# Transposed-tile copies moved from ScalarE to VectorE in the attention stage, and two-bank PSUM tiles with paired GELUs in the first FFN stage

## The chip, the cores and the metric

The kernel runs on all 8 cores of one Trainium2 chip. The batch of 32 sequences is split into 4 per core, and the cores share nothing else than HBM. The metric is the device time in microseconds of the slowest core. A core has five engines that run side by side: TensorE (PE, with its weight loads shown as PEld), VectorE (DVE), ScalarE (ACT), GpSimd (POOL, here only a queue for DMAs) and SyncE (SP, also a queue for DMAs). They order each other by semaphores.

## The reference

For x of shape (32, 2048, 1024), in float32, one layer is computed:

```
h   = layernorm(x)
u   = h @ W_in.T + b_in ;  s_t = exp(lambda_log) * s_(t-1) + gamma * u_t     (scan over 2048 steps)
att = s @ W_out.T + b_out + h
x   = x + layernorm(att)
z   = quant_act(layernorm(x)) @ quant_weight(w1).T        (1024 -> 4096, weights in {-1,0,1} * scale)
y   = quant_act(gelu(z)) @ quant_weight(w2).T             (4096 -> 1024)
out = x + layernorm(y)
```

`quant_act` scales each row by 127 over its largest magnitude and rounds, so the largest magnitude of a row must be known before any of its elements is quantised.

## The kernel before

The program has four phases one after the other, each a block with its own code for every engine.

Phase 0 transposes W_in and W_out on TensorE and copies the results out of PSUM with VectorE (`winT`, `woutT`).

Phase A (lines 277 to 747) is the attention part, in 32 blocks of 256 tokens (two tiles of 128). Each engine runs through the blocks in an order written out by hand.

- VectorE, block b: the statistics of x (`bn_stats`, tile `bn`), then `attnp(b-1)`: attention output plus residual (`attn_b`, from PSUM tile `ps_a`) and its statistics (`bn6a`, `bn2a`), then `r2p(b-1)`: the residual sum `r2b`, its statistics and its largest magnitude (`am3s`), then `scans_sec(b)`: eight scans (`ybf`, the recurrence over 256 tokens of 128 channels each), then up to three tasks of the weight quantisation (`dve_qslot(3)`: `qrtmp` for the mean, later `t1b`, `t2b` for the three-valued weights). There are 68 such tasks, so they fill blocks 0 to 22.
- ScalarE, block b: four tiny operations and `ln1f` for each of the two tiles, then four copies `lnT<-ps_t` (the transposed, normalised input, four 128x128 transposes at a time), then `ln2p(b-1)`: four tiny operations and `t2buf` for each tile, which `r2p(b-1)` on VectorE waits for, then eight `gu` (PSUM `ps_u` to SBUF, one for each scan), then `ln3p(b-1)`.
- TensorE, block b: `mm2sec(b-1)` (`ps_a`, four groups of one bias matmul, L701, and eight matmuls, L705), then 16 transposes in four groups (`ps_t`, L726; the third group waits until the first copy is done, since `ps_t2` has two buffers), then 64 matmuls `ps_u` (L738) in eight groups, each of which waits for the `gu` two before it.

Phase B1 (lines 749 to 917) is the first FFN matmul with GELU and quantisation, in 64 tiles of 128 tokens. TensorE computes eight 512-column slices `ps_h` (eight matmuls each, L914), into six one-bank PSUM tiles in turn. ScalarE applies GELU to each slice into the single buffer `h_b` (128x4096). VectorE takes the row maximum of the whole `h_b` (`tensor_reduce`, tile `amh`), forms the scale (`sch_all`), then runs `dcorr(ta+1)`, which ends with the quantised input `qd` of the next tile, and then the quantisation of this tile (`bh`, `ch`, `bh`, `qh_b`), for which it waits for ScalarE's `y0h` and `r16h`. SyncE transposes `qd` by DMA into `qdT`, and TensorE waits for that. So TensorE can't start tile ta+1 before the row maximum of tile ta is done. The helper at L148 issues every VectorE and ScalarE operation, and for that reason most rows carry that line.

Phase B2 (lines 919 to 1029) is the second FFN matmul, with a last layernorm. The change does not touch it.

The copies as they stand before, on ScalarE:

```python
a.wait_ge(sem("s_lt"), grp + 1)
if b >= 2:
    a.wait_ge(sem("s_u"), DT * (b - 1))
ie = a.activation(lTv[b % 2][:, 4 * q:4 * q + 4, 128 * tt:128 * (tt + 1)],
                  ps_t2[grp % 2][:].rearrange("p (q r) -> p q r", q=4),
                  AF.Identity, bias=zerov[:], scale=1.0)
inc("s_lte", ie)
```

Of the kernel before, what the change touches and what calls it, by code (L numbers as in the profile page):

```python
# [7 lines left out]
F32 = mybir.dt.float32  # L8
# [11 lines left out]
def build_program(NB=4, L=2048, D=1024, H=4096, TA=256,  # L20
                  phases=("0", "A", "B1", "B2"), acap=None, dbgqd=False):
    DT = D // 128
# [31 lines left out]
    with es:  # L54
# [51 lines left out]
        def sem(n):  # L106
            return sems[n][0]
# [169 lines left out]
        with contextlib.ExitStack() as pA:  # L277
# [98 lines left out]
            def _(v):  # L376
# [120 lines left out]
                for b in range(NBLKA):  # L497
                    seg = b % SEGB
                    for t in range(TPB):
                        ta = TPB * b + t  # L500
                        v.wait_ge(sem(f"sxA{b % 2}"), 16 * (b // 2 + 1))
                        if ta >= 2:
                            v.wait_ge(sem("s_ln1"), ta - 1)
                        v.bn_stats(bn6[:, 0:6], x_buf[b % 2][:, t * D:t * D + 512])
                        v.bn_stats(bn6[:, 6:12], x_buf[b % 2][:, t * D + 512:t * D + 1024])
                        ia0 = v.bn_aggr(bn2[ta % 2][:], bn6[:])
                        inc("s_st0", ia0)
                    if b >= 1:
                        attnp(b - 1)
                    if b >= 1:  # L510
                        r2p(b - 1)
                    scans_sec(b)
                    dve_qslot(3)
# [5 lines left out]
            def _(a):  # L519
# [33 lines left out]
                for b in range(NBLKA):  # L553
                    for t in range(TPB):
# [17 lines left out]
                        inc("s_ln1", i1)  # L572
                    for gi in range(GPB):
                        grp = GPB * b + gi
                        tt = gi // (DT // 4)
                        q = gi % (DT // 4)
                        a.wait_ge(sem("s_lt"), grp + 1)
                        if b >= 2:
                            a.wait_ge(sem("s_u"), DT * (b - 1))
                        ie = a.activation(  # L580
                            lTv[b % 2][:, 4 * q:4 * q + 4, 128 * tt:128 * (tt + 1)],
                            ps_t2[grp % 2][:].rearrange("p (q r) -> p q r", q=4),
                            AF.Identity, bias=zerov[:], scale=1.0)
                        inc("s_lte", ie)
                    if b >= 1:
# [163 lines left out]
        with contextlib.ExitStack() as p1:  # L749
            def sb1(name, shape, dt):  # L750
# [17 lines left out]
            tnt = sb1("tnt", [128, NT], F32)  # L768
            ps_h = [p1.enter_context(nc.psum_tensor(f"ps_h{i}", [128, 512], F32))
                    for i in range(6)]  # L770
            blk = p1.enter_context(nc.Block())
# [33 lines left out]
            def _(v):  # L805
# [28 lines left out]
                for ta in range(NT2):  # L834
                    v.wait_ge(sem("s_gel"), HS * ta + HS)
                    v.tensor_reduce(amh[:], h_b[:], axis=AX.X,
# [23 lines left out]
            def _(a):  # L860
                a = _Proxy(chains["a"], a)
                a.wait_ge(sem("s_pre"), 1)
                for it in range(NT2 + 1):
# [12 lines left out]
                    if it >= 1:  # L876
                        tb = it - 1
                        for hs in range(HS):
                            q = HS * tb + hs
                            a.wait_ge(sem("s_h3"), q + 1)  # L880
                            ig = a.activation(h_b[:, 512 * hs:512 * (hs + 1)],
                                              ps_h[q % 6][:], AF.Gelu,
                                              bias=zerov[:], scale=g3s[:, tb:tb + 1])
                            inc("s_gel", ig)
# [19 lines left out]
            def _(t):  # L904
                t.wait_ge(sem("s_w1T"), 16)
                for ta in range(NT2):
                    t.wait_ge(sem(f"s_qdT{ta % 2}"), 16 * (ta // 2 + 1))
                    for hs in range(HS):
                        q = HS * ta + hs
                        if q >= 6:  # L910
                            t.wait_ge(sem("s_gel"), q - 5)
                        last = None
                        for j in range(DT):
                            last = t.matmul(ps_h[q % 6][:],  # L914
                                            qdTv[ta % 2][:, j, :],
# [158 lines left out]
```

## Time and profile before

| | |
|---|---|
| median of the runs | 4552.75 us (4550.93 to 4554.58, 2 runs) |
| the profiled execution | 4520.1 us, span of its slowest core (core 2) 4518.6 us |
| spans of the eight cores | 4497.7 to 4518.6 us |
| phase A, core 2 | about 57.6 to 1582 us |
| phase B1, core 2 | 1599 to 3582 us |
| phase B2, core 2 | 3619 to 4518.6 us |
| busy over the span | PE 63%, DVE 63%, ACT 39%, POOL 4% |

Times in a profile are microseconds from the start of the span. A busy share is an average over phases with different limits, so each phase is read by itself. The timeline of one block or one tile shows which engine each operation waited for: the brackets at the end of a row give the idle time before it and what released it. The granted clock of TensorE ("PEclk") is given as a share of full speed: 1.00 is 2.4 GHz, 0.50 is 1.2 GHz, and a value between is a mean over the two levels.

### The profile page before, as it was taken

To read this page: it belongs to the slowest core of one execution; us is meant where nothing else is said; L and a number is where in the kernel's file an instruction comes from. 1 tells how busy PE (TensorE), PEld (TensorE's weight loads), DVE (VectorE), ACT (ScalarE), POOL (GpSimd) and SP (SyncE) were. 2 spreads that over 40 slices of the span, in tenths; PEclk is the share of its full clock that TensorE was granted. 3 is DMA by queue.
4 is the path that set the end of the run, shared out by engine and by line. 5 is a ranking of instruction groups with operands and counts; after the bars stand their busy time and mean duration, and the time that the engine had idled before them with its cause. 6 is when DMAs were issued, how large, how long until landed. Compare 5 with 4: busy or idle time off the path is not lost. (4 is left out here: it accounts for less than half of the span.)

```text
span 4518.6 us, 40554 instructions; the slowest of 8 cores (4497.7 to 4518.6 us)
## 1 busy us (share of the span) xinstructions
PE 2841.8 (63%) x12080; PEld 1570.2 (35%) x12080; DVE 2852.6 (63%) x2500; ACT 1761.6 (39%) x2181; POOL 201.5 (4%) x372
## 2 busy tenths in 40 slices
PE   5565655555667445545545545545545299999998
PEld 4454444444455312212212212222222144444444
DVE  4666666667665558878878878788888522222322
ACT  1434333333454344554555555555555211111111
POOL 0000000000000000000000000000000000000000
PEclk7766666667787778778777777777777699999999
DMA  4332346566411212122122122122122366666665
GB/s 131 112 112 89 113 127 159 136 165 162 114 59 52 103 61 63 52 65 63 52 65 63 51 65 63 51 65 63 55 62 64 114 143 154 153 150 155 152 153 127
DMA packets 537185, 447.33 MB, mean 99 GB/s; under 512 B 473206, under 2 KB 473208, under 8 KB 524424
## 3 DMA queue, kind: packets, MB, share of 16 engines
q1 hardware_dynamic: 479624, 184.58, 18.1%
q0 software_dynamic: 57344, 260.15, 17.1%
q8 instruction: 100, 1.64, 0.2%
q14 instruction: 117, 0.96, 0.1%
HBM read 193.02 MB, written 151.00 MB: 76 GB/s over the span
## 5 line engine op out<-in xcount | busy, mean ns | idle before, releaser
L914 PE MATMUL ps_h<-w1T,qdT 128*128 128x512 bf16 x4096 | 1032.4, 419 | 972.5 <-DMA qdT<-qd 972.5
L914 PEld LDWEIGHTS ps_h<-w1T,qdT 128*128 128x128 bf16 x4096 | 429.1, 106 | 1575.7 <-issue 1188.7
L1026 PE MATMUL ps_f<-w2T,qhT 128*128 128x512 bf16 x4096 | 886.4, 380 | 69.0 <-DMA qhT<-qhscr 69.0
L148 ACT ACTIVATE h_b<-ps_h,zerov,g3s 128x512 f32<-128x512 f32 x512 | 397.9, 777 | 569.1 <-PE ps_h L914 569.1
L738 PE MATMUL ps_u<-lnT,winT 128*128 128x256 f32 x2048 | 411.6, 382 | 304.8 <-ACT gu L148 267.1
L1026 PEld LDWEIGHTS ps_f<-w2T,qhT 128*128 128x128 bf16 x4096 | 401.2, 98 | 554.2 <-issue 72.3
L738 PEld LDWEIGHTS ps_u<-lnT,winT 128*128 128x128 f32 x2048 | 389.0, 289 | 331.9 <-issue 330.7
L148 DVE BATCH_NORM_STATS2 bn<-ffn 128x6 f32<-128x512 f32 x128 | 88.8, 694 | 575.3 <-ACT ffn L148 568.4
L148 DVE TENSOR_TENSOR bh<-y0h,r16h 128x4096 bf16<-128x4096 f32 x64 | 283.2, 4426 | 209.0 <-ACT r16h L148 209.0
L148 ACT ACTIVATE y0h<-h_b,halfv,sch_all 128x4096 f32<-128x4096 f32 x64 | 243.2, 3800 | 358.3 <-DVE sch_all L148 358.3
L148 DVE TENSOR_REDUCE amh<-h_b 128x1 f32<-128x4096 f32 x64 | 282.9, 4420 | 124.3 <-ACT h_b L148 124.3
L705 PE MATMUL ps_a<-woutT,ybf 128*128 128x512 f32 x1024 | 318.3, 460 | 0.0
L148 ACT ACTIVATE ffn<-ps_f,zerov,g4s 128x1024 f32<-128x1024 f32 x64 | 77.0, 1203 | 598.8 <-PE ps_f L1026 598.7
L148 ACT ACTIVATE gu<-ps_u,gbv,vecs 128x256 f32<-128x256 f32 x256 | 144.4, 564 | 381.5 <-DVE ybf L148 285.1
L148 DVE SCALAR_TENSOR_TENSOR ch<-y0h,r16h 128x4096 bf16<-128x4096 f32 x64 | 283.2, 4425 | 6.7
L148 DVE SCALAR_TENSOR_TENSOR qh_b<-r16h,bh 128x4096 bf16<-128x4096 int16 x64 | 283.2, 4425 | 6.6
L726 PE MATMUL ps_t<-identt,ln1f 128*128 128x128 f32 x512 | 105.9, 371 | 233.2 <-ACT ln1f L148 184.5
L705 PEld LDWEIGHTS ps_a<-woutT,ybf 128*128 128x128 f32 x1024 | 212.5, 218 | 78.0 <-issue 35.1
L148 ACT ACTIVATE r16h<-y0h,zerov 128x4096 int16<-128x4096 f32 x64 | 237.3, 3707 | 5.9
L148 DVE TENSOR_TENSOR_SCAN ybf<-lam_bc,ybf,gu 128x256 fp32r<-128x256 f32 x224 | 168.1, 751 | 100.5 <-ACT gu L148 84.0
L726 PEld LDWEIGHTS ps_t<-identt,ln1f 128*128 128x128 f32 x512 | 83.3, 192 | 256.7 <-issue 254.0
L148 DVE TENSOR_TENSOR r2b<-t2buf,x_buf 128x1024 f32<-128x1024 f32 x64 | 78.4, 1225 | 138.0 <-ACT t2buf L148 133.9
(99 smaller groups left out, 2407.7 us busy)
## 6 DMA issues: line engine op xcount, KB each, us to landing
qstg<-w SPq DMA_DIRECT2D x64, 1024.0 KB, 6.5
qhscr<-qh_b POOLq DMA_DIRECT2D x64, 1024.0 KB, 5.1
x_buf<-x POOLq DMA_DIRECT2D x32, 1024.0 KB, 6.3
r2scr<-r2b POOLq DMA_DIRECT2D x64, 512.0 KB, 2.9
r2B<-r2scr POOLq DMA_DIRECT2D x64, 512.0 KB, 5.8
r2C<-r2scr POOLq DMA_DIRECT2D x64, 512.0 KB, 5.5
y<-outb POOLq DMA_DIRECT2D x64, 512.0 KB, 2.9
w1tscr<-wtp SPq DMA_DIRECT2D x32, 256.0 KB, 3.0
```

Source lines behind the costliest of these rows:

```text
L148: ins = f(*a, **k)
L705: last = t.matmul(pslice, ybv[b % 2][:, k, 128 * tt:128 * (tt + 1)], wov[:, k, 512 * half:512 * (half + 1)], start=False, stop=(k == DT - 1))
L726: mm = t.transpose(ps_t2[grp % 2][:, 128 * r:128 * (r + 1)], ln1f[b % 2][:, tt * D + 128 * dd:tt * D + 128 * (dd + 1)], identt[:])
L738: last = t.matmul(ps_u[gcnt % 2][:], wiv[:, j, 128 * k:128 * (k + 1)], lTv[b % 2][:, j, :], start=(j == 0), stop=(j == DT - 1))
L914: last = t.matmul(ps_h[q % 6][:], qdTv[ta % 2][:, j, :], w1v[:, j, 512 * hs:512 * (hs + 1)], start=(j == 0), stop=(j == DT - 1))
L1026: last = t.matmul(pslice, qhTv[ta % 2][:, j, :], w2v[:, j, 512 * half:512 * (half + 1)], start=(j == 0), stop=(j == HT - 1))
```

## The change

Two edits that have nothing to do with each other.

In phase A the four copies `lnT<-ps_t` of a block leave ScalarE, where they stood between `ln1f` and `ln2p(b-1)`, and go to VectorE, between `attnp(b-1)` and `r2p(b-1)`, as `tensor_copy` with the same waits and the same semaphore.

In phase B1 PSUM is cut into four tiles of two banks (1024 columns) instead of six of one. TensorE still writes 512 columns per group, alternately into the first and the second half. ScalarE runs one GELU over 1024 columns once both halves are done, four per tile instead of eight. The counts of the waits follow.

```diff
@@ phase A, VectorE
                     if b >= 1:
                         attnp(b - 1)
+                    for gi in range(GPB):
+                        grp = GPB * b + gi
+                        tt = gi // (DT // 4)
+                        q = gi % (DT // 4)
+                        v.wait_ge(sem("s_lt"), grp + 1)
+                        if b >= 2:
+                            v.wait_ge(sem("s_u"), DT * (b - 1))
+                        ie = v.tensor_copy(
+                            lTv[b % 2][:, 4 * q:4 * q + 4, 128 * tt:128 * (tt + 1)],
+                            ps_t2[grp % 2][:].rearrange("p (q r) -> p q r", q=4))
+                        inc("s_lte", ie)
                     if b >= 1:
                         r2p(b - 1)
@@ phase A, ScalarE: the same loop with a.activation(..., AF.Identity, ...) is taken out
@@ phase B1
-            ps_h = [p1.enter_context(nc.psum_tensor(f"ps_h{i}", [128, 512], F32))
-                    for i in range(6)]
+            ps_h = [p1.enter_context(nc.psum_tensor(f"ps_h{i}", [128, 1024], F32))
+                    for i in range(4)]
@@ VectorE
-                    v.wait_ge(sem("s_gel"), HS * ta + HS)
+                    v.wait_ge(sem("s_gel"), (HS // 2) * (ta + 1))
@@ ScalarE
-                        for hs in range(HS):
-                            q = HS * tb + hs
-                            a.wait_ge(sem("s_h3"), q + 1)
-                            ig = a.activation(h_b[:, 512 * hs:512 * (hs + 1)],
-                                              ps_h[q % 6][:], AF.Gelu,
+                        for hp in range(HS // 2):
+                            q = HS * tb + 2 * hp
+                            a.wait_ge(sem("s_h3"), q + 2)
+                            ig = a.activation(h_b[:, 1024 * hp:1024 * (hp + 1)],
+                                              ps_h[(q // 2) % 4][:], AF.Gelu,
@@ TensorE
-                        if q >= 6:
-                            t.wait_ge(sem("s_gel"), q - 5)
+                        if q >= 8:
+                            t.wait_ge(sem("s_gel"), q // 2 - 3)
+                        pslot = ps_h[(q // 2) % 4][:, 512 * (q % 2):512 * (q % 2 + 1)]
-                            last = t.matmul(ps_h[q % 6][:],
+                            last = t.matmul(pslot,
```

## Rows read from the trace of the kernel before

**Rows 1.** Windows: stretch, us; busy us (count) of PE, PEld, DVE, ACT, POOL; PEclk; DMA
```profile
57.60:1221.90 1164.30, 670.94 (x2748) 539.18 (x2748) 770.67 (x945) 451.11 (x894) 42.81 (x71) 0.68 0.46 130
```

**Rows 2.** Waits, 57.6 to 1221.9 us: total us, times, longest (blocks 1 to 23)
```profile
PE ps_t L726 <- ACT ln1f L148: 184.5, 22, 21.9
DVE r2b L148 <- ACT t2buf L148: 104.6, 23, 4.9
```

**Rows 3.** Waits, 1221.9 to 1535.7 us (blocks 24 to 31)
```profile
DVE attn_b L148 <- PE ps_a L705: 41.1, 16, 5.6
DVE r2b L148 <- ACT t2buf L148: 29.3, 8, 3.9
```

**Rows 4.** Timeline, block 14: start us, length us, engine, work, [idle before <-releaser]
```profile
732.66 1.94 PE L726 MATMUL ps_t<-identt,ln1f 128*128 128x128 f32 x8 [1.70 <-ACT lnT L148]
...
733.89 0.21 DVE L148 BATCH_NORM_AGGREGATE bn2a<-bn6a 128x2 f32<-128x12 f32 x1
733.95 0.69 ACT L148 ACTIVATE lnT<-ps_t,zerov 128x512 fp32r<-128x512 f32 x1 [0.66 <-PE ps_t L726]
...
734.81 0.69 ACT L148 ACTIVATE lnT<-ps_t,zerov 128x512 fp32r<-128x512 f32 x1 [0.17 <-ACT lnT L148]
...
735.59 0.29 ACT L148 ACTIVATE lnv<-bn2a,epsv 128x1 f32<-128x1 f32 x1
...
738.71 1.23 DVE L148 TENSOR_TENSOR r2b<-t2buf,x_buf 128x1024 f32<-128x1024 f32 x1 [4.61 <-ACT t2buf L148]
```

**Rows 5.** Timeline, block 26
```profile
1307.34 1.47 ACT L148 ACTIVATE lnT<-ps_t,zerov 128x512 fp32r<-128x512 f32 x2 [2.61 <-PE ps_t L726]
...
1309.01 1.47 ACT L148 ACTIVATE lnT<-ps_t,zerov 128x512 fp32r<-128x512 f32 x2 [0.20 <-ACT lnT L148]
...
1309.86 0.21 DVE L148 BATCH_NORM_AGGREGATE bn2a<-bn6a 128x2 f32<-128x12 f32 x1
...
1313.69 1.23 DVE L148 TENSOR_TENSOR r2b<-t2buf,x_buf 128x1024 f32<-128x1024 f32 x1 [3.62 <-ACT t2buf L148]
```

**Rows 6.** Groups by line and form: busy us, mean ns of one
```profile
L148 ACT ACTIVATE h_b<-ps_h,zerov,g3s 128x512 f32<-128x512 f32 x512 | 397.9, 777 | 569.1 <-PE ps_h L914 569.1
...
L148 ACT ACTIVATE lnT<-ps_t,zerov 128x512 fp32r<-128x512 f32 x128 | 87.9, 687 | 65.0 <-PE ps_t L726 52.2 <-ACT lnT L148 6.7
...
L148 ACT ACTIVATE ffn<-ps_f,zerov,g4s 128x1024 f32<-128x1024 f32 x64 | 77.0, 1203 | 598.8 <-PE ps_f L1026 598.7
...
L148 DVE CAST winT<-ps_t 128x512 fp32r<-128x512 f32 x16 | 11.1, 691 | 4.3 <-PE ps_t L224 3.5 <-DVE winT L148 0.2
```

**Rows 7.** Timeline, one tile of phase B1, its TensorE block and its end
```profile
2428.58 16.11 PE L914 MATMUL ps_h<-w1T,qdT 128*128 128x512 bf16 x64 [14.54 <-DMA qdT<-qd]
...
2444.84 0.78 ACT L148 ACTIVATE h_b<-ps_h,zerov,g3s 128x512 f32<-128x512 f32 x1 [0.95 <-PE ps_h L914]
...
2445.79 4.42 DVE L148 TENSOR_REDUCE amh<-h_b 128x1 f32<-128x4096 f32 x1 [1.58 <-ACT h_b L148]
```

**Rows 8.** Tile amh, whole program: count, duration ns min/median/max, first and last start
```profile
L148 DVE TENSOR_REDUCE amh<-h_b x64: 4419/4420/4421, 1616.3 to 3551.9; 128x1 f32<-128x4096 f32 x64
```

**Rows 9.** Timeline, VectorE, a delayed tile of phase B1 and those after it
```profile
1831.33 4.42 DVE L148 TENSOR_REDUCE amh<-h_b 128x1 f32<-128x4096 f32 x1 [1.66 <-ACT h_b L148]
...
1862.51 4.42 DVE L148 TENSOR_REDUCE amh<-h_b 128x1 f32<-128x4096 f32 x1 [2.12 <-ACT h_b L148]
...
1893.00 4.42 DVE L148 TENSOR_REDUCE amh<-h_b 128x1 f32<-128x4096 f32 x1 [1.42 <-ACT h_b L148]
...
1923.61 4.42 DVE L148 TENSOR_REDUCE amh<-h_b 128x1 f32<-128x4096 f32 x1 [1.55 <-ACT h_b L148]
```

**Rows 10.** Windows, PE: first 5 us of two TensorE blocks; busy, PEclk, DMA, GB/s
```profile
1814.05:1819.05 5.00, 5.00 (x13) 0.55 0.02 3
1845.14:1850.14 5.00, 5.00 (x14) 0.59 0.00 0
```

**Rows 11.** Timeline, PE, first matmul group of mm2sec, blocks 27 and 28
```profile
1334.49 2.11 PE L705 MATMUL ps_a<-woutT,ybf 128*128 128x512 f32 x8
...
1372.20 3.78 PE L705 MATMUL ps_a<-woutT,ybf 128*128 128x512 f32 x8
```

More of the change, by code:

```diff
@@ L572, in _ @@
                         inc("s_ln1", i1)
[L573 to L584, printed above, removed]
                     if b >= 1:
```

## The prediction, before the change was run

> **What bounds the kernel now.** I cut the span into its phases by the windows view first, because the page's busy shares are means over phases with different limits. Then I read the waits of phase A, in two halves, the timeline of one block in each half, and the timeline of one tile of phase B1. Phase B2 is left alone: the change doesn't touch it.
>
> Phase A, blocks 1 to 23. VectorE is busy 770.7 of 1164.3 us [rows 1], and what is left of its time is mostly waiting. TensorE waits for `ln1f` in 22 blocks [rows 2], which itself waits for VectorE's statistics, so TensorE is behind VectorE and not ahead of it. VectorE does its work in one line: scans, quantisation tasks, statistics, `attnp`, then a wait for ScalarE's `t2buf` (23 times, 104.6 us, so 4.55 us in each block [rows 2]), then `r2p`, then the scans of the next block. The reader is to see in the timeline why that wait is there: `attnp` ends at 733.89 + 0.21 = 734.10, but ScalarE is still copying `lnT` (until 735.50) and starts its `ln2p` at 735.59 only; `r2b` starts at 738.71 [rows 4]. The four copies that the change moves stand ahead of the very operation that VectorE waits for.
>
> Phase A, blocks 24 to 31, has no quantisation tasks. The line is the same except that `attnp` now also waits for TensorE's `mm2sec` (16 times, 41.1 us), and the wait for `t2buf` is 29.3/8 = 3.66 us [rows 3].
>
> Phase B1. 64 tiles take (3551.9 - 1616.3)/63 = 30.72 us each [rows 8]. The loop that closes is: row maximum, `dcorr` of the next tile, DMA transpose, TensorE's block of 16.1 us, last GELU, row maximum. VectorE waits 1.58 us for the last GELU [rows 7], so its own work is 1.58 us shorter than the loop. TensorE waits for `qdT` and never for a free PSUM tile, so six banks or eight makes no difference to it.
>
> **The change in phase A.** One copy costs 687 ns on ScalarE and 691 ns on VectorE for exactly this shape and type (`winT` in phase 0) [rows 6], so the work itself costs the same. The Trainium skill, "VectorE: DVE Perf Modes", section on the TRN2 errata, gives PSUM to SBUF as 120 cycles plus columns at 0.96 GHz for VectorE and 172 plus columns at 1.2 GHz for ScalarE: as an estimate, 658 against 570 ns, 88 ns dearer for the move, which over 31 blocks of four would take 11 us off the gain below. The two rows don't bear that difference out.
>
> What the copies cost on VectorE's line in blocks 1 to 23: VectorE is free at 734.10 and the first two groups of transposes have been done for a while, so copy 1 starts at 734.2, ends at 734.9, and copy 2 follows. The third group of transposes starts about 0.14 us after copy 1, at 735.03. From its start to copy 3 was 733.95 - 732.66 = 1.29 us, and to copy 4 another 734.81 - 733.95 = 0.86 us [rows 4]; so copy 3 starts at 736.32, copy 4 at 737.18, and it ends at 737.87. `r2b` can start at 737.97. ScalarE meanwhile starts `ln2p` as soon as the statistics are there, and needs 738.71 - 735.59 = 3.12 us for the first tile [rows 4]. The first tile's statistics were done before the second's, which began at 733.89, so the first `t2buf` is there by 737.0 at the latest, before VectorE asks for it. The second follows by 740.2 at the latest and is wanted when VectorE is through `r2b`, the statistics and the maximum of the first tile. So the copies go into a wait that they themselves had caused: 3.87 us of work in a wait of 4.61, gain 0.74 us a block. Over 23 blocks that is -17.0 us.
>
> Blocks 24 to 31: VectorE is free at 1309.86 + 0.21 = 1310.07, the four copies took 1309.01 + 1.47 - 1307.34 = 3.14 us on ScalarE [rows 5], so `r2b` would start at about 1313.4 instead of 1313.69: -0.3 us a block, -2.2 us over eight. But TensorE sits idle for 3 us in the middle of its transposes, and if its clock falls there they take as long as in block 14, which makes it 3.87 us and +0.4 us a block, +3 us. I take 0 for these eight blocks, with -2 and +3 as bounds. What queues behind the new waits on VectorE is `r2p` and then the scans; POOL's store of `r2b` and its load of the next x wait for `r2p` and move with it. On TensorE the `ps_u` matmuls start 2.4 us later, since copy 4 ends at 737.87 and not at 735.50. What needs them first is `gu`, wanted when the scans begin, and between lies the whole of `r2p` on VectorE, two tiles of which `r2b` alone is 1.23 us each. Were that cover gone, 2.4 us a block would show, 74 us in all.
>
> **The change in phase B1.** Four GELUs in place of eight save issue on ScalarE, which waits for TensorE between them anyway: nothing. The last GELU of a tile is on the loop. It takes 777 ns now. A 1024-column one of the same source and the same kind of scale takes 1203 ns (`ffn`) [rows 6]. It starts as before when TensorE's last group is done, so the row maximum comes 0.426 us later, and nothing hides it: VectorE is already waiting there [rows 7]. Taken plainly this is 64 x 0.426 = +27.3 us.
>
> I don't think it stays so. The block of TensorE starts slow and turns fast. In a usual tile, granted clock 0.55 in its first 5 us, 4.5 us were at 1.2 GHz; in a block that started 0.37 us late (1845.14, against 1814.05 + 30.72) the mean was 0.59, so 4.1 us at 1.2 GHz [rows 10]. A late start shortened the slow stretch by about as much as it was late, and so the block by half of it. The row maxima show the same from outside: after the delayed tile (31.18 us) the next took 30.49 and 30.61 us [rows 9], so that of 0.46 us late 0.23 and then 0.12 were left. Lateness halves from tile to tile. If every tile adds 0.426, the lateness settles where half of it is 0.426, at 0.85 us, once for the phase and not per tile, and the period stays 30.72. The slow stretch would then be 4.5 - 0.85 = 3.6 us. The rows show this down to 4.1 us only.
>
> The Trainium skill, "TensorE: Matmul & The Clock Gate", section "What's actually happening", says that the monitor behind the clock runs freely and doesn't start anew with the work. By that rule the slow stretch ends at a moment that lateness doesn't move, and rows 10 agree. The same section's note on the warm-up, taken as a fixed time from the first matmul, speaks against this change: each tile would keep its slow stretch and pay the full 27.3 us.
>
> **Sum.** The profiled execution took 4520.1 us, 32.7 below the median of the runs. Blocks 1 to 23 -17.0, blocks 24 to 31 0, phase B1 +0.9: -16, so 4504 for an execution like the profiled one, and 4552.75 - 16 = 4537 for the median. Bounds: phase A from -19 to 0, phase B1 from +0.9 to +27.3.
>
> **The rivals.**
>
> 1. The longer GELU is paid in every tile. For it: VectorE waits exactly there, and no row shows a slow stretch under 4.1 us. Against it: rows 9 and 10. It decides for slower as soon as more than 17 of the 27.3 us are kept, that is if TensorE gives back less than 0.16 us a tile. Place: the time between two row maxima, 31.15 instead of 30.72. Time: 4552.75 - 17.0 + 27.3 = 4563.
>
> 2. TensorE's clock in blocks 24 to 31. A group of eight matmuls of `mm2sec` takes 2.11 us at the fast level and 3.78 at the slow one, as it did in block 28 [rows 11], and in these blocks VectorE waits for `mm2sec` [rows 3]. Three or four slow groups cost 5.0 to 6.7 us a block. The move leaves a longer idle stretch in TensorE's block. If four more of the eight blocks meet the 1.2 GHz level there, +24 us: 4561. If the ones that meet it today no longer do, some 12 us less: 4525. Nothing in the profile says which block gets the slow level, so this is a spread on either side more than a direction.
>
> 3. VectorE has no room and the copies lie on its line in full: 31 x 3.87 = +120 us, 4672. This is what a look at the page alone suggests, since VectorE is the busiest engine with ScalarE at 39%. Against it: the wait of 4.55 us in all 23 blocks is caused by the work that is moved. It needs `t2buf` to come no earlier than today.
>
> **How the numbers follow.** Forecast as above 0.66, rival 1 0.14, rival 2 upwards 0.08 and downwards 0.08, rival 3 0.04. The likeliest gives 4537. The range for 8 in 10 takes in both sides of rival 2, rival 1, and a few us by which the runs differ: 4518 to 4566. A measurement of this kernel tells about 2% from no change, which is 91 us. Only rival 3 leaves that band: slower 0.04, faster 0.01, same 0.95.
>
> **What would show it.** Phase A: `r2b` waits under 0.5 us instead of 4.55, its start in a block relative to the end of the scans before is 0.7 us earlier, VectorE's copies take 0.69 us. If `r2b` still waits for `t2buf`, the step on ScalarE is wrong. Phase B1: a GELU of 1.20 us, and the distance of two row maxima either 30.72 (lateness given back, PEclk in the first 5 us of a block about 0.64) or 31.15 (rival 1, PEclk 0.55). VectorE's wait there stays 1.6 us by the forecast and is 2.0 by rival 1. The forecast is wrong above all if the slow stretch can't be shortened below what rows 10 show.

## The result, and the profile after

| | median of the runs | ratio to before, 95% interval |
|---|---|---|
| before, beside the changed kernel | 4538.55 us (42 runs) | |
| after | 4513.86 us (43 runs) | 0.9938 (0.9917 to 0.9958) |

The medians are over all executions, while the ratio leaves out those in which the cores of one die ran slower at a lower clock. So the change takes 0.6% off: 24.7 us between the medians, and 28 us (19 to 38) by the ratio, which is within 2% of no change, as forecast with 0.95. The forecast was 16 us off, to 4537, in a range of 4518 to 4566. The direction and the mechanism in blocks 1 to 23 held. The time lies 4.1 us below the range. Of the 38.9 us between the 4552.75 that stood as the time before and the 4513.86 after, 14.2 aren't the change's: the median of two runs was 4552.75, and of 42 runs it is 4538.55.

The spans of the eight cores come first, because they say which core to read.

```profile
core 0: 4530.4 us, clock 0.789
core 1: 4505.7 us, clock 0.792
core 2: 4491.2 us, clock 0.792
core 3: 4472.4 us, clock 0.794
...
```

The slowest core of the profiled execution is core 0. In it and in core 1 there were two stretches of 165 to 200 us in phase B1 in which TensorE's blocks ran at a lower granted clock; phase B1 took 2014 and 2012 us there, against 1981 to 1984 on the other six. The two rows below are whole blocks of core 0 by the windows view (us, PE busy, PEclk, DMA share, GB/s): 17.81 us at 0.76 and, outside such a stretch, 15.29 us at 0.88. Such stretches fall on pairs of neighbouring cores, also where the code is that of before: in the profiled execution of "the order on ScalarE" below phase B2 took 1000 and 1005 us on cores 0 and 1, against 938 to 945 on the others. So I take them for a disturbance and not for an effect of the change. I read the changed kernel on core 2, and sums over phase A as means over all eight cores.

```profile
2123.69:2141.50 17.81, 17.72 (x63) 0.76 0.04 16
2290.61:2305.90 15.29, 15.24 (x62) 0.88 0.00 1
```

Phase A, the timeline of block 14 on core 2, to be held against [rows 4]:

```profile
724.85 0.29 ACT L148 ACTIVATE lnv<-bn2a,epsv 128x1 f32<-128x1 f32 x1
...
726.77 1.24 ACT L148 ACTIVATE t2buf<-attn_b,bias,rstd2c 128x1024 f32<-128x1024 f32 x1
726.91 0.21 DVE L148 BATCH_NORM_AGGREGATE bn2a<-bn6a 128x2 f32<-128x12 f32 x1
727.22 1.49 DVE L148 CAST lnT<-ps_t 128x512 fp32r<-128x512 f32 x2
...
728.06 1.94 PE L725 MATMUL ps_t<-identt,ln1f 128*128 128x128 f32 x8 [4.09 <-DVE lnT L148]
...
729.39 0.69 DVE L148 CAST lnT<-ps_t 128x512 fp32r<-128x512 f32 x1 [0.68 <-PE ps_t L725]
...
730.25 0.69 DVE L148 CAST lnT<-ps_t 128x512 fp32r<-128x512 f32 x1 [0.17 <-DVE lnT L148]
731.04 1.23 DVE L148 TENSOR_TENSOR r2b<-t2buf,x_buf 128x1024 f32<-128x1024 f32 x1
```

The order is as predicted. `ln2p` of the first tile (`t2buf`, 726.77) runs before VectorE has begun the copies, the copies take 0.69 us each, and `r2b` starts right behind them with no bracket, so it waits for nothing. From the start of the second tile's aggregation to `r2b` it is 731.04 - 726.91 = 4.13 us; before it was 738.71 - 733.89 = 4.82 [rows 4]. In the waits of blocks 1 to 23 the 104.6 us for `t2buf` [rows 2] have gone:

```profile
DVE r2b L148 <- DVE lnT L148: 0.5, 1, 0.5
PE ps_t L725 <- DVE lnT L148: 99.0, 23, 5.0
DVE lnT L148 <- PE ps_t L725: 21.0, 25, 3.8
```

In their place TensorE waits 99.0 us in the middle of its transposes, where nobody waits for it but the copies.

Phase B1, core 2: the row maxima of the whole program, then the first matmuls of a tile's block and the end of it in the timeline, and the granted clock in the first 5 us of that block and the next.

```profile
L148 DVE TENSOR_REDUCE amh<-h_b x64: 4419/4420/4421, 1588.9 to 3524.8; 128x1 f32<-128x4096 f32 x64
```

```profile
2309.30 15.69 PE L914 MATMUL ps_h<-w1T,qdT 128*128 128x512 bf16 x64 [14.99 <-DMA qdT<-qd]
...
2325.14 1.20 ACT L148 ACTIVATE h_b<-ps_h,zerov,g3s 128x1024 f32<-128x1024 f32 x1 [2.25 <-PE ps_h L914]
...
2326.52 4.42 DVE L148 TENSOR_REDUCE amh<-h_b 128x1 f32<-128x4096 f32 x1 [1.61 <-ACT h_b L148]
```

```profile
2309.30:2314.30 5.00, 5.00 (x16) 0.65 0.00 0
2339.95:2344.95 5.00, 5.00 (x16) 0.64 0.00 0
```

The period is (3524.8 - 1588.9)/63 = 30.73 us, against 30.72 [rows 8], though the last GELU takes 1.20 us where it took 0.78. The block shrank from 16.11 [rows 7] to 15.69 us, and VectorE's wait is 1.61 against 1.58.

### The profile page after: what moved, and what is told of

Same layout as the page of the kernel before. It is cut to its first block and busy times, and to the rows that moved or that the text cites. A ratio compares the mean times of both kernels' runs of the same rounds, so it can differ in the third digit from the quotient of the medians.

```text
span 4530.4 us, 39620 instructions; the slowest of 8 cores (4472.4 to 4530.4 us)
## 1 busy us (share of the span) xinstructions
PE 2786.8 (62%) x11916; PEld 1545.9 (34%) x12080; DVE 2941.2 (65%) x2628; ACT 1583.9 (35%) x1797; POOL 201.5 (4%) x372
## 5 line engine op out<-in xcount | busy, mean ns | idle before, releaser
L148 ACT ACTIVATE h_b<-ps_h,zerov,g3s 128x1024 f32<-128x1024 f32 x256 | 308.1, 1204 | 690.9 <-PE ps_h L914 690.9
L737 PE MATMUL ps_u<-lnT,winT 128*128 128x256 f32 x2048 | 392.3, 373 | 223.4 <-ACT gu L148 185.7
L737 PEld LDWEIGHTS ps_u<-lnT,winT 128*128 128x128 f32 x2048 | 378.7, 283 | 243.2 <-issue 240.6
L704 PE MATMUL ps_a<-woutT,ybf 128*128 128x512 f32 x1024 | 287.7, 426 | 0.0
L704 PEld LDWEIGHTS ps_a<-woutT,ybf 128*128 128x128 f32 x1024 | 193.2, 199 | 68.5 <-issue 31.4
L148 DVE TENSOR_TENSOR bh<-ch,bh 128x4096 bf16<-128x4096 bf16 x64 | 146.7, 2292 | 7.0 <-DVE ch L148 0.5
```

What stands on the lines that cost most here:

```text
L148: ins = f(*a, **k)
L704: last = t.matmul(pslice, ybv[b % 2][:, k, 128 * tt:128 * (tt + 1)], wov[:, k, 512 * half:512 * (half + 1)], start=False, stop=(k == DT - 1))
L737: last = t.matmul(ps_u[gcnt % 2][:], wiv[:, j, 128 * k:128 * (k + 1)], lTv[b % 2][:, j, :], start=(j == 0), stop=(j == DT - 1))
```

## Where the time went

From the timelines of all eight cores, one profiled execution of each kernel, means over the cores in us:

| stretch | before | after | difference | forecast |
|---|---|---|---|---|
| blocks 1 to 23 | 1120.0 | 1103.9 | -16.1 | -17.0 |
| of it, second `attnp` to `r2b` | 177.5 | 162.4 | -15.1 | -17.0 |
| blocks 24 to 31 | 306.2 | 300.8 | -5.4 | 0 |
| of it, the groups of `mm2sec` | 65.4 | 59.7 | -5.7 | 0 |
| of it, second `attnp` to `r2b` | 54.3 | 56.1 | +1.8 | -2 to +3 |
| start of TensorE in phase B1 (time from the span's start) | 1584.3 | 1560.0 | -24.3 | |
| phase B1, from there to the last `qh_b` | 1982.2 | 1982.7 | +0.5 | +0.9 |

The groups of `mm2sec` are taken from the start of the first to the start of the fourth in each block. The value of B1 after is that of cores 2 to 7, which differ among themselves by 3 us. The differences of blocks 1 to 23 and of blocks 24 to 31 leave -2.8 of the -24.3: about -0.9 in block 0 and -1.9 between the last scan and phase B1, which the prediction didn't name. The rows that it got wrong are the third and the fourth, that is the groups of `mm2sec` in blocks 24 to 31.

## The experiments

The two edits were split first. Then the two places where TensorE's clock answers to the change (late blocks of phase A, tiles of phase B1) were each driven on their own. Last, the wait that the change had found was attacked in another way.

### The copies alone

```diff
 # phase B1 as before; of the change only
+    for gi in range(GPB): ... v.tensor_copy(lTv[...], ps_t2[grp % 2]...)   # VectorE
-    for gi in range(GPB): ... a.activation(lTv[...], ps_t2[grp % 2]...)    # ScalarE
```

> Only the copies of phase A go to VectorE; phase B1 is that of before. Theory A (the gain of the change lies in phase A, because the copies fill a wait that they had caused): the wait of VectorE for t2buf is under 0.5 us a block instead of 4.55, the start of r2b moves 0.66 us ahead in blocks 1 to 23, phase B1 keeps a period of 30.72 us, and the whole is 15 to 30 us faster than before, ratio 0.993 to 0.997. Rival (most of the gain comes from phase B1, by fewer GELU instructions): at most 10 us faster, ratio above 0.998.

4500.01 against 4541.93 us, ratio 0.9913 (0.9873 to 0.9953). Blocks 1 to 23 took 1102.0 us and blocks 24 to 31 300.8, means over the cores, as with the whole change. By the ratio that is 40 us (21 to 58), more than the 15 to 30 expected, though the interval takes in part of them. On core 2 `r2b` waits once, for 0.5 us, and the stretch from the second `attnp` to `r2b` shrinks by 0.66 us a block in the mean of the cores, as expected. The interval overlaps the whole change's, so the copies carry all of the gain that can be measured.

### The GELU alone

Phase A is that of before; of phase B1, the PSUM tiles and all waits are those of the change. The excerpt shows ScalarE's part.

```diff
-            a.wait_ge(sem("s_h3"), q + 1)
-            ig = a.activation(h_b[:, 512 * hs:512 * (hs + 1)], ps_h[q % 6][:], AF.Gelu,
+            a.wait_ge(sem("s_h3"), q + 2)
+            ig = a.activation(h_b[:, 1024 * hp:1024 * (hp + 1)], ps_h[(q // 2) % 4][:], AF.Gelu,
```

> Only the paired GELUs of phase B1; phase A is that of before. Theory A (the longer last GELU, 0.43 us, makes each TensorE block start late, and the block gives it back by a shorter stretch at 1.2 GHz): the period of two row maxima stays 30.72 us, PEclk in the first 5 us of a block is about 0.64, the time is that of before within 0.1% (ratio 0.999 to 1.001). Rival (the longer GELU is paid in each tile): period 31.15 us, PEclk 0.55, +27 us, ratio 1.006.

4541.39 us, ratio 1.0007 (0.9968 to 1.0046). The mean period is 30.72 to 30.74 us on all eight cores; here core 4.

```profile
L148 DVE TENSOR_REDUCE amh<-h_b x64: 4420/4420/4421, 1591.4 to 3527.2; 128x1 f32<-128x4096 f32 x64
```

Rival 1 asked for 27.3 us, which is 0.6% and outside the interval, and no core shows its mean period of 31.15 us.

### Less work on the loop

If the period is held by the moment at which TensorE gets to 2.4 GHz, and not by the sum of the work, then work taken off the loop must change nothing either.

```diff
-    v.tensor_scalar(amh[:], amh[:], EPS, None, op0=ALU.max)
-    v.reciprocal(irc[:], amh[:])
-    i3 = v.tensor_scalar(sch_all[:, ta:ta + 1], irc[:], 127.0, None, op0=ALU.mult)
+    v.tensor_scalar(amh[:], amh[:], 1.0 / 127.0, EPS / 127.0, op0=ALU.mult, op1=ALU.max)
+    i3 = v.reciprocal(sch_all[:, ta:ta + 1], amh[:])
```

> Before, with one tiny VectorE operation (0.25 us with its gap) taken off the loop of phase B1: the lower bound EPS and the factor 127 go into one operation ahead of the reciprocal, so the scale of a row differs in rounding only. Theory A (the loop is held at 30.72 us by the moment at which TensorE gets to 2.4 GHz, from both sides): the period stays 30.72 us although the loop's work is 0.25 us shorter, each TensorE block starts earlier and spends about 0.5 us more at 1.2 GHz (PEclk in its first 5 us near 0.50 instead of 0.55), time unchanged, ratio 0.999 to 1.001. Rival (a loop in which each term counts): period 30.47 us, 16 us faster, ratio 0.9965.

4535.32 us, ratio 0.999 (0.9943 to 1.0037). The row maxima of core 4, and the first 5 us of a block:

```profile
L148 DVE TENSOR_REDUCE amh<-h_b x64: 4419/4420/4421, 1591.6 to 3527.4; 128x1 f32<-128x4096 f32 x64
```

```profile
2035.04:2040.04 5.00, 5.00 (x12) 0.50 0.00 0
```

Again 30.73, where a loop in which each term counts asked for 30.47. (The interval of the time takes in both, so the row maxima decide.) The 0.25 us went into a longer stretch at 1.2 GHz, which now fills the first 5 us (0.50), and VectorE's wait rose to 1.9 us.

### More work on the loop: one, two and five small operations

In the first two the GELUs are in pairs and phase A is as before; in the third the GELUs are single. Each added line costs about 0.26 us and repeats an operation without effect on the result. "Added to before" in the table below counts from before, so the pair's 0.43 us is in it.

```diff
     v.tensor_scalar(amh[:], amh[:], EPS, None, op0=ALU.max)
+    v.tensor_scalar(amh[:], amh[:], EPS, None, op0=ALU.max)   # once, twice, five times
```

> The paired GELUs of phase B1 alone, with one more tiny VectorE operation on the loop (the bound EPS a second time, which changes nothing in the result, 0.26 us with its gap): 0.68 us added to the loop of before. Theory A: period still 30.72 us, 64 x 0.68 = 44 us of added work free of charge, PEclk in the first 5 us of a TensorE block about 0.69 (slow stretch 3.1 us). Rival (paid in each tile once the slow stretch has reached the 3.6 us of the changed kernel): period 30.98 us.

> As the run before with two more such operations: 0.94 us added to the loop of before. Theory A has a limit here: no block in the traces so far, of any phase, got to 2.4 GHz less than about 2.8 us after a start at 1.2 GHz, and this loop would need 2.6. So lateness can't be given back in every tile any more: some tiles pay a whole longer stretch at 1.2 GHz, and the mean period lies clear above 30.72, between 31.2 and 31.7 us, with tiles of very different length. Rival (the slow stretch can shrink on, without limit): 30.72 in every tile. Second rival (each added us is simply paid): 31.66 in every tile, evenly.

> Before (single GELUs) with five more such operations on the loop of phase B1: 1.28 us added. Theory A with the limit: uneven tiles, mean period 31.6 to 32.0 us. Rival (simply paid): even tiles of 32.0 us. Rival without limit: 30.72 us.

I read these by their row maxima, since each is a single execution. The four rows are one operation more on core 6 and on core 1, two on core 2, five on core 2.

```profile
L148 DVE TENSOR_REDUCE amh<-h_b x64: 4419/4420/4421, 1617.2 to 3554.1; 128x1 f32<-128x4096 f32 x64
```

```profile
L148 DVE TENSOR_REDUCE amh<-h_b x64: 4419/4420/4421, 1590.4 to 3531.7; 128x1 f32<-128x4096 f32 x64
```

```profile
L148 DVE TENSOR_REDUCE amh<-h_b x64: 4419/4420/4421, 1596.3 to 3572.7; 128x1 f32<-128x4096 f32 x64
```

```profile
L148 DVE TENSOR_REDUCE amh<-h_b x64: 4419/4420/4421, 1614.9 to 3627.9; 128x1 f32<-128x4096 f32 x64
```

Together with the earlier kernels:

| kernel | added to before | period | at 1.2 GHz in a usual block |
|---|---|---|---|
| one operation less | -0.25 | 30.73 | 5.0 or more |
| before | 0 | 30.72 | 4.5 |
| after, and the GELU alone | +0.43 | 30.73 | 3.5 |
| one operation more | +0.68 | 30.74 (core 6), 30.81 to 30.83 (five cores) | 3.1 |
| two more | +0.94 | 31.37 to 31.43 | changes |
| five more | +1.28 | 31.95 to 32.03 | changes |

The last column is worked out from PEclk in the first 5 us: the share below 1, times two, times 5 us; 0.50, 0.55, 0.65 and 0.69 give 5.0, 4.5, 3.5 and 3.1. The usual tile, by the median of all 64, keeps 30.71 to 30.74 us over 0.93 us of work. But at +0.68 us that is only just so. The cores other than core 6 each had one or two tiles of 32.6 to 32.7 us, the first of them with three tiles behind it that were still too long (31.4, 31.1 and 30.9), so five of them come to 30.81 to 30.83 in the mean. (Cores 4 and 5, at 31.11 and 31.07, also had a disturbed stretch.) The expectation of 30.72 held for the usual tile, then, and not for the sum: some 5 us of the 44 were paid. The rival's 30.98 in every tile shows on no core. In the steady state each 0.43 us added shortens the stretch at 1.2 GHz by about twice that, and the block by half of the latter: the rule that the prediction had from two blocks of before.

With two operations more the period is no longer held, and the trace shows how it goes. TensorE's first 5 us in five blocks that follow each other on core 2, and VectorE's wait at the row maximum in the same tiles:

```profile
2704.16:2709.16 5.00, 5.00 (x18) 0.74 0.00 0
2734.89:2739.89 5.00, 5.00 (x18) 0.74 0.01 3
2765.63:2770.63 5.00, 5.00 (x12) 0.50 0.00 0
2798.04:2803.04 5.00, 4.78 (x13) 0.57 0.00 0
2829.64:2834.64 5.00, 5.00 (x16) 0.66 0.00 0
```

```profile
2720.94 4.42 DVE L148 TENSOR_REDUCE amh<-h_b 128x1 f32<-128x4096 f32 x1 [1.17 <-ACT h_b L148]
...
2751.66 4.42 DVE L148 TENSOR_REDUCE amh<-h_b 128x1 f32<-128x4096 f32 x1 [1.15 <-ACT h_b L148]
...
2784.08 4.42 DVE L148 TENSOR_REDUCE amh<-h_b 128x1 f32<-128x4096 f32 x1 [2.83 <-ACT h_b L148]
...
2815.66 4.42 DVE L148 TENSOR_REDUCE amh<-h_b 128x1 f32<-128x4096 f32 x1 [1.99 <-ACT h_b L148]
...
2846.82 4.42 DVE L148 TENSOR_REDUCE amh<-h_b 128x1 f32<-128x4096 f32 x1 [1.31 <-ACT h_b L148]
```

The slow stretch shrinks to 2.6 us (0.74), and the next block falls back to the whole 5 us at 1.2 GHz (0.50). That tile takes 2784.08 - 2751.66 = 32.42 us. The following ones are still longer than 30.72, each time by about half as much (31.58, then 31.16), while the slow stretch shortens again (0.57, 0.66), until it happens anew. The expectation set the limit at about 2.8 us; here blocks still turned fast after 2.6. With five operations more it happens every second or third tile, and the mean of 31.95 is 30.72 + 1.23: almost all of the added 1.28 us is paid, though in uneven tiles and not in even ones.

### The late blocks of phase A: work added

The blocks 24 to 31 had gained 5.4 us where I had put 0. The theory was that the copies' work made the block longer and so led TensorE past its 1.2 GHz level. Then any work of that size must do it, without the copies moving.

```diff
+    if b >= 23 and t == 0:
+        v.bn_aggr(bn2r[ta % 2][:], bn6r[:])
```

> Before, with one tiny VectorE operation more (a second bn_aggr with the same result, 0.31 us with its gap) in the first tile of r2p in the last blocks of phase A. In the changed kernel blocks 26 to 31 took 37.53 to 37.55 us each and no core met a 1.2 GHz mm2sec in full, whereas before they took 37.2 to 37.4 and nearly every core met one block of 44 us. Theory A (the small rise of the period, and not the place of the copies, is what keeps mm2sec at 2.4 GHz): with 0.31 us more work a block, the blocks take about 37.5 us, the 44 us blocks vanish on most cores, and blocks 24 to 31 take about 302 us in the mean of the eight cores instead of 306, so added work makes them faster. Rival (the 44 us blocks come by chance or by what else runs on TensorE): they stay in most cores, and the eight blocks take about 308 us.

Blocks 24 to 31 took 301.1 us, mean over the cores, against 306.2 before and 300.8 after: with 0.31 us of work added per block they are 5.1 us shorter. In before, six of eight cores had a block of about 44 us among blocks of mostly 37.2 to 37.4 (core 2 had two), core 4 had one of 42.5 and core 7 none. In this kernel, in after and with the copies alone no core has one; with the latter two, blocks 26 to 31 take 37.51 to 37.55 us each, and here 37.4 to 37.9.

This is one execution, so chance has to be asked. Four kernels of this document with the late blocks as before and no disturbed core there (one operation less, one more, and the two with the correction ahead) took 303.6 to 308.0 us in them, and 22 of their 32 cores had a block of about 44. With before that makes 29 of 40 cores, against none of 24 in the three kernels with the longer block. So the blocks of 44 us don't stay away by chance; the size of the gain is uncertain, 2.5 to 6.9 us against those four.

The difference is the speed of `mm2sec`. Here are the first and the last of its four groups in a late block of this kernel (core 3), and then block 28 of before (core 2, whose first group is in [rows 11]):

```profile
1371.10 0.47 PE L703 MATMUL ps_a<-bout_r,ones_rr 1*128 1x512 f32 x1 [2.02 <-DVE ybf L148]
1371.50 2.11 PE L707 MATMUL ps_a<-woutT,ybf 128*128 128x512 f32 x8
...
1378.89 2.12 PE L707 MATMUL ps_a<-woutT,ybf 128*128 128x512 f32 x8
```

```profile
1371.51 0.76 PE L701 MATMUL ps_a<-bout_r,ones_rr 1*128 1x512 f32 x1 [2.02 <-DVE ybf L148]
...
1376.64 3.78 PE L705 MATMUL ps_a<-woutT,ybf 128*128 128x512 f32 x8
...
1381.07 3.78 PE L705 MATMUL ps_a<-woutT,ybf 128*128 128x512 f32 x8
...
1385.32 2.12 PE L705 MATMUL ps_a<-woutT,ybf 128*128 128x512 f32 x8
```

With all groups at the fast level the section takes 1378.89 + 2.12 - 1371.10 = 9.91 us, with three of four at the slow level 1385.32 + 2.12 - 1371.51 = 15.93. Those 6.0 us are most of what sets a block of 44.21 us apart from one of 37.3. In block 24 single first groups still ran slow (3.4 to 3.7 us), on four cores of this kernel and on four of after.

### The order on ScalarE, copies left where they were

The wait that the change removes is caused by order: `ln2p` stands behind four copies. Putting the first tile's `ln2p` ahead of them should free VectorE without giving it work.

```diff
-                def ln2p(b):
-                    for t in range(TPB):
+                def ln2p(b, ts=None):
+                    for t in (range(TPB) if ts is None else ts):
@@ ScalarE, block b
+                    if b >= 1:
+                        ln2p(b - 1, [0])
                     for gi in range(GPB): ...        # the four copies
-                        ln2p(b - 1)
+                        ln2p(b - 1, [1])
```

> Before, with one change on ScalarE in phase A: ln2p of the first tile stands ahead of the four copies, which stay on ScalarE, and ln2p of the second tile stays behind them. Theory A (VectorE waits for t2buf only because the copies stand ahead of it): r2b of the first tile starts within 0.3 us of the end of attnp, which takes away 3 to 4.5 us a block without any work for VectorE; the second tile's t2buf may then come about 1 us late in the blocks with quantisation tasks. Gain 2.5 to 3.5 us in each of 31 blocks, 80 to 110 us, ratio 0.976 to 0.983. Rival (the next limit is right behind: the scans wait for gu, because ps_u begins later): the scans of a block take longer by what r2b gained, and the whole gains less than 30 us, ratio above 0.993.

4490.95 us, ratio 0.9871 (0.9802 to 0.9941). Block 14 on core 6:

```profile
687.77 1.24 ACT L148 ACTIVATE t2buf<-attn_b,bias,rstd2c 128x1024 f32<-128x1024 f32 x1
688.19 0.21 DVE L148 BATCH_NORM_AGGREGATE bn2a<-bn6a 128x2 f32<-128x12 f32 x1
...
689.10 1.47 ACT L148 ACTIVATE lnT<-ps_t,zerov 128x512 fp32r<-128x512 f32 x2
689.25 1.23 DVE L148 TENSOR_TENSOR r2b<-t2buf,x_buf 128x1024 f32<-128x1024 f32 x1 [0.84 <-ACT t2buf L148]
```

From the second aggregation to `r2b` it is 1.06 us here, 4.82 before and 4.13 after. (I had expected `r2b` within 0.3 us of the end of `attnp`; it still waits 0.84.) In blocks 1 to 23 the stretch from the second `attnp` to `r2b` shrank from 177.5 to 91.0 us, that is 3.76 a block. The second tile's `t2buf` now stands behind the copies, so 1.28 a block came back between `r2b` and the first scan (250.7 to 280.1). Waits of blocks 1 to 23:

```profile
DVE r2b L148 <- ACT t2buf L148: 52.0, 46, 1.7
DVE ybf L148 <- ACT gu L148: 87.1, 84, 12.2
```

Blocks 1 to 23 are 57.6 us shorter and blocks 24 to 31 23.9, means over the cores, though every core has one or two blocks of 40.4 to 40.7 us among late blocks of 33.7 to 36.0: the slow `mm2sec` is back with the shorter block. The last scan ends 83 us earlier, within the 80 to 110 I expected. By the ratio the kernel is 58 us faster (27 to 90), where 0.976 to 0.983 was expected and the interval takes in only a part of it; cores 0 and 1, with their disturbed phase B2, are the slowest of the profiled execution by 40 us. The move to VectorE gained little more than a fourth of this (16.1 of 57.6 in blocks 1 to 23) because it refills with copies most of the wait that it empties.

### Phase B1, the correction two tiles ahead

The loop of B1 closes over `dcorr` of the next tile. Made for the tile after next, it leaves TensorE's block of the next tile free to run beside VectorE's work.

```diff
+                dcorr(1)
                 for ta in range(NT2):
                     ...
-                    if ta + 1 < NT2:
-                        dcorr(ta + 1)
+                    if ta + 2 < NT2:
+                        dcorr(ta + 2)
```

(The loads of `r2B` and ScalarE's preparation go one tile ahead with it; the GELUs are in pairs.)

> Phase B1 of the changed kernel, with the quantised input made one tile earlier: in tile ta VectorE runs dcorr(ta+2) instead of dcorr(ta+1), ScalarE and the loads run one tile ahead. TensorE no longer waits for the row maximum, and with eight banks it can run almost a tile ahead. Phase A is that of before. Theory A (VectorE is the next limit, 1.6 us under today's period): period 29.1 us, the wait for h_b vanishes, the wait for r16h stays 3.2 us, 64 x 1.6 = 103 us faster, ratio 0.977. Rival (TensorE, which now works in other stretches, or ScalarE holds the loop): period 30.7 us and a wait for h_b of more than 1 us stays.

Ratio 0.9781 (0.9751 to 0.9812), where 0.977 was expected; the profiled execution took 4426.86 us.

```profile
L148 DVE TENSOR_REDUCE amh<-h_b x64: 4419/4420/4421, 1617.3 to 3456.1; 128x1 f32<-128x4096 f32 x64
```

```profile
DVE bh L148 <- ACT r16h L148: 168.9, 53, 3.2
```

The period is 29.19 us, and the wait for the GELU has gone. What ends last now is ScalarE's `r16h`, for which VectorE waits 3.2 us a time (the second fence, waits of 1650 to 3200 us, 53 times). The next kernel hands `r16h` over in two halves and lets VectorE work in halves (the first of its four operations is shown; the other three, and ScalarE's `y0h` and `r16h`, are halved likewise):

```diff
-                    v.wait_ge(sem("s_r16h"), ta + 1)
-                    v.tensor_tensor(bh[:], y0h[ta % 2][:], r16h[ta % 2][:], op=ALU.is_lt)
+                    for hh in range(2):
+                        hsl = slice(hh * H // 2, (hh + 1) * H // 2)
+                        v.wait_ge(sem("s_r16h"), 2 * ta + hh + 1)
+                        v.tensor_tensor(bh[:, hsl], y0h[ta % 2][:, hsl],
+                                        r16h[ta % 2][:, hsl], op=ALU.is_lt)
```

> As e9, and y0h, r16h and the four quantisation operations of VectorE run in two halves of 2048 columns. Theory A (VectorE's wait of 3.2 us for r16h is the time to the whole of it; the first half is there after 4.2 us, while dcorr takes 4.5): the wait is under 0.3 us, four more fixed costs of about 0.15 us each come back, period about 26.5 us, 64 x 4.2 = 270 us faster than before, ratio 0.940. Rival (the two engines or ScalarE's own line of 16 us slow each other down): period above 28 us.

4294.95 us, ratio 0.9485 (0.9461 to 0.951).

```profile
L148 DVE TENSOR_REDUCE amh<-h_b x64: 4419/4420/4422, 1611.2 to 3322.1; 128x1 f32<-128x4096 f32 x64
```

The phase by windows (busy us of PE, PEld, DVE, ACT, POOL; PEclk, DMA), and one operation of its timeline:

```profile
1611.00:3327.00 1716.00, 1011.21 (x4026) 420.66 (x4024) 1604.53 (x1007) 965.23 (x627) 65.57 (x123) 0.79 0.22 67
```

```profile
2409.48 2.29 DVE L148 TENSOR_TENSOR bh<-y0h,r16h 128x2048 bf16<-128x2048 f32 x1
```

The period is 27.16 us and the wait for `r16h` is gone. That is 0.7 above what I expected: a half costs 2.29 us, and two of them 0.15 more than the 4.43 of the whole, besides a gap more for each. VectorE is busy 1604.53 of 1716.00 us, so this loop is now bound by VectorE's own work.

### Both: the order of phase A, and phase B1 in halves

The edits of "the order on ScalarE" and of the last kernel in one; no new lines.

> Phase A of e4 (copies on ScalarE, ln2p of the first tile ahead of them) with phase B1 of e10. Theory A (the phases are independent, so the gains add): about 80 us from phase A as in the trace of e4, 270 us from phase B1, ratio 0.92 to 0.93. Rival (the gains do not add, for example because phase B2 or the clock pays back): ratio above 0.94.

4217.78 us, ratio 0.932 (0.9299 to 0.934): 6.8% off before, and faster than the changed kernel by six points. The gains add, with the ratio at the edge of the 0.92 to 0.93 expected: the last scan ends 85 us earlier than before (83 with the order alone), and phase B1 is 227 us shorter, as in halves alone.

## Why the prediction was right or wrong

**The copies in blocks 1 to 23: right, slightly too large.** `r2b` waits for nothing, the copies take 0.69 us, the work on ScalarE was ready in time, and TensorE's later `ps_u` cost nothing. The stretch gave 15.1/23 = 0.66 us a block instead of 0.74. The schedule written out for block 14 was met almost row by row: copy 1 starts 727.22 - 727.12 = 0.10 us after the aggregation ends, as assumed, and from copy 1 to `r2b` it is 731.04 - 727.22 = 3.82 us against 737.97 - 734.2 = 3.77. That leaves 0.69 for block 14, and the mean over blocks and cores is 0.03 less again. With what the rest of these blocks gave, the term was 0.9 us too large.

**Blocks 24 to 31: wrong, the largest error of the sum.** The step that failed is "I take 0 for these eight blocks"; they gave -5.4 us. The part that it worked out, the copies' own cost, came at +0.22 us a block, inside its bounds. (Its upper value of +0.4 is a slip: 3.87 us of copies in a wait of 3.62 make +0.25.) What it left to a rival was TensorE's clock in `mm2sec`. Rival 2 downwards, with a chance of 0.08, is what happened, on seven cores of eight. Its price of 12 us was that of core 2, which had lost two blocks, and the mean core had lost one: -5.7. The reason given for not choosing a side was that "nothing in the profile says which block gets the slow level". The experiment with 0.31 us of added work shows that a slightly longer block keeps it away on all cores. Before, at 37.2 to 37.4 us, it met eight blocks of 64; at 37.51 to 37.55 it never did, and with the order changed, at 33.7 to 36.0, it met every core. So the length of the blocks bears on whether `mm2sec` falls on the slow level. The prediction's price came from core 2 alone. The other cores of the same trace had one such block or none, and core 7, which had none, took 299.1 us for the eight blocks: that was the size of the downward side. Why 37.53 us is a period that avoids it isn't settled by these runs.

**Phase B1: right.** The step "lateness halves from tile to tile ... the period stays 30.72" gave 0.65 for PEclk (0.64 forecast), a wait of 1.61 (1.6), and +0.5 us for the phase (+0.9). It rested on two blocks of the trace and a shrinkage seen only down to 4.1 us. The experiments carry it to 3.5 us without a loss and to 3.1 with the first single tiles that break, and show its end at 2.6. Rival 1 had 0.14; something like it, paid in uneven tiles, comes true 0.5 us of work later. The Trainium skill, "TensorE: Matmul & The Clock Gate", section "What's actually happening", says of the monitor behind the clock that "it doesn't reset when your kernel starts". The traces agree: at four amounts of work from -0.25 to +0.68 us the usual tile keeps one period.

**Ends of phase A: not in the sum.** Block 0 and the tail after the last scan gave -2.8 us. The prediction had no term for either, and no run takes them apart, so their cause stays open.

**The baseline: not in the range.** All numbers of the range were sums of mechanisms on top of 4552.75, which was the median of two runs. Its own profiled execution took 4520.1, 32.7 less, and the prediction says so, but takes "a few us by which the runs differ". The 14.2 us between the medians of two and of 42 runs is more than the error of the mechanisms, which is -24.7 + 16 = -9. The time missed the range by 4.1 us, so without the one or the other it would have been inside. That the baseline was too high is luck of two executions and no fault of a mechanism, but a range built on two runs should have allowed for it.

**Rival 3** (the copies in full, +120 us) is refuted by every kernel with the copies on VectorE.

## What to carry over

Before moving work to the busiest engine, look at what that engine waits for: if it waits for the very engine that is relieved, the move fits into its own wait. But then ask first whether the order on the donor alone does it, because that leaves the wait empty; here it was worth more than twice as much as the move. Where a loop has one TensorE block that begins at 1.2 GHz, small savings and small costs on the loop show up in the clock and not in the time; a cost shows in full only beyond what the slow stretch can take up (here nothing was paid up to +0.43 us, a little at +0.68), and a gain needs a change of the loop's shape, or a larger saving than the 0.25 us tried here, for which no run shows where the period gives way.

## What was not expected of the hardware

- A period that holds against work. From -0.25 to +0.43 us of work per tile the period stayed 30.72 to 30.74 us. At +0.68 us one or two tiles of 64 took 32.6 to 32.7 us on seven cores of eight, and at +0.94 us tiles of 32.4 us came every few tiles: it breaks in single tiles, and not by a slow growth.
- Added work that makes a stretch faster: 0.31 us more in each of eight blocks made them 5.1 us shorter together, because no `mm2sec` ran at 1.2 GHz beyond its first group.
- In the blocks of 44 us `mm2sec` begins at 1.2 GHz and stays there through 13 us of matmuls that follow each other without an idle time in the trace, three groups of 3.78 us, and is at 2.4 GHz only in the fourth (2.12 us). In block 24 of some cores it begins there too and is at 2.4 GHz from the second group on, so a slow start alone doesn't settle how long it lasts.
- ScalarE pays little for width: a GELU with its scale from a tile takes 777 ns at 512 columns [rows 6] and 1205 at 1024 (mean of the 256 in the changed kernel), so a pair costs 349 ns less than two singles. The 1203 ns that the forecast used were those of `ffn`, a plain scaling of the same width, and came within 2 ns.
